# Attention and feed-forward layer on eight cores: one PSUM copy goes to another engine, one wait moves behind the state update

## The chip, the cores and the metric

The kernel runs on all 8 cores of one Trainium2 chip. Each core takes one of the 8 sequences of the batch, with no traffic between cores. The time is the device time of the slowest core, in microseconds; of several runs the median counts.

## The reference

`x` has the shape (8, 8192, 1024). The layer computes, all in float32:

```python
q, k, v = x @ Wq.T, x @ Wk.T, x @ Wv.T          # 8 heads of 128
# causal linear attention without softmax, in chunks:
inter  = q_chunk @ state
scores = (q_chunk @ k_chunk.T) * tril
intra  = scores @ v_chunk
state  = state + k_chunk.T @ v_chunk
o = (inter + intra) / max(|q . cumsum(k)|, 1)
o = rmsnorm(o, norm_w, per head) @ Wo.T
x = layernorm(x + o)
# feed-forward with 8-bit fake-quantised weights and a rank-16 addition
h = gelu(x @ (quant(W_fc) + 2 * B_fc @ A_fc).T + b_fc)
y = h @ (quant(W_proj) + 2 * B_proj @ A_proj).T + b_proj
x = layernorm(x + y)
```

## The kernel before

The program is written for each engine by hand. A small class `Prog` holds one list of instructions per engine and one counting semaphore per engine (`pe`, `ve` for DVE, `ac` for ACT, `gd` and `ld` for the DMAs). `P.wait(engine, token)` puts a wait into that engine's list, `P.op` and `P.close` give the token of an instruction. Every engine works through its list strictly in order, so whatever stands behind a wait waits too. The order of each list is the order in which the Python code emits it.

Pass 1 does the attention. It loops over 16 tiles of 512 rows (`for t in range(NT1)`). Each tile has two phases.

In the first, `qkv_groups` makes 24 groups of eight matmuls (L275 for q and k, L298 for v; 128x512 each) into the three PSUM banks pR0, pR1 and pD, copied out in turns by ACT (L287, L310) and DVE (L284, L307). From the fifth group on, one step of the tail of the tile before is emitted behind each group: `s_sq` (squares on ACT, L322, sums on DVE, L325), `s_dn` (the denominators), then for each of four blocks of 128 rows `s_apply` (L360, DVE scales the block into osq) and `s_wo`. In `s_wo` TensorE transposes the block into pZ (L376) and pSA (L383), two copies bring it to `o2f_sb` (L388 and L391), and TensorE multiplies it by Wo (L401, eight matmuls into pOA and eight into pOB), which waits for both copies. L408 and L412 (DVE) add the input. `s_ssq` (L431, ACT) follows.

In the second phase four chunks of 128 rows pass through the state recurrence. For each chunk TensorE transposes k (L556, into pR0 and pR1) and computes the scores (L565, into pSA and pSB). ACT copies the transposed k to `ktm_sb` (L572, L574). DVE masks the scores (L577, L579) and casts the float32 state to bf16 (L584, token `t_scpy`, `state_f32` to `state_sb`). TensorE then computes the state update from `ktm_sb` and `v_sb` (L595, eight matmuls into pR0 and pR1; L601, the key sums, into pZ), which DVE adds to `state_f32` (L606, L610, L614), and the output of the chunk: q times state (L627, L632), masked scores times v (L641, L647). ACT copies the output (L655, L657, L659). Behind it the late steps of the tile before are emitted: the layer-norm scalars (`s_ln`: DVE L442 to L459, ACT L455) behind chunk 0 and one output each (`s_out`: ACT L469) behind chunks 1, 2 and 3, and one job that finds the maximum of a slice of the feed-forward weights (DMA L247, DVE L249 and L252).

Behind pass 1 the feed-forward weights are quantised while the feed-forward tiles begin (from L763 on), and 32 tiles of 256 rows run through two matmuls (L935, L953). Neither edit touches that part.

Of the kernel before, what the change touches and what calls it, by code (L numbers as in the profile page):

```python
# [77 lines left out]
def later(*toks):  # L78
    out = {}
    for t in toks:  # L80
        if t is None:
            continue
        if isinstance(t, list):
            for tt in t:
                if tt is not None:
                    s, v = tt
                    out[s] = max(out.get(s, -1), v)
            continue
        s, v = t
        out[s] = max(out.get(s, -1), v)  # L90
    return [(s, v) for s, v in out.items()]


def build_program(S=8192, debug=False):
# [32 lines left out]
    P = Prog()  # L127
# [56 lines left out]
    with contextlib.ExitStack() as s1:  # L184
# [27 lines left out]
        pSA, pSB = ps1("pSA"), ps1("pSB")  # L212
# [7 lines left out]
        for Wbuf, Wd in [(WqT, wqT_d), (WkT, wkT_d), (WvT, wvT_d), (WoT, woT_d)]:  # L220
# [10 lines left out]
        fr = {"pR0": None, "pR1": None, "pOA": None, "pOB": None, "pD": None,  # L231
              "pSA": None, "pSB": None, "pZ": None, "ostg": None,
              "o2f": None, "sTm": None,
              "scales": None,
              "ktm": None, "state": None, "osq": [None, None],
              "xtm": [None, None], "r1": [None] * 4, "x1o": [None, None],
              "wst": None, "o1rd": [None, None]}
# [77 lines left out]
        def make_tail(t, xb, oev_toks, dn_toks, msq_gate):  # L315
# [53 lines left out]
            def s_wo(j):  # L369
                def f():  # L370
                    P.wait("tensor", fr["apl", j])
                    P.wait("tensor", fr["o2f"])
                    P.wait("tensor", fr["pZ"])
                    for hh in range(4):
                        P.em("tensor", lambda e, h_=hh, c4=hh:
                             e.matmul(pZ[:, c4 * 128:c4 * 128 + 128],  # L376
                                      osq_sb[j % 2][:, h_ * 128:h_ * 128 + 128],
                                      ident16[:], start=True, stop=True))
                    tk0 = P.close("tensor", "pe")
                    P.wait("tensor", fr["pSA"])  # L380
                    for hh in range(4):
                        P.em("tensor", lambda e, h_=4 + hh, c4=hh:
                             e.matmul(pSA[:, c4 * 128:c4 * 128 + 128],  # L383
                                      osq_sb[j % 2][:, h_ * 128:h_ * 128 + 128],
                                      ident16[:], start=True, stop=True))
                    tk1 = P.close("tensor", "pe")
                    P.wait("scalar", tk0)
                    fr["pZ"] = P.op("scalar", "ac", lambda e: e.copy(  # L388
                        o2f_sb[:, 0:512], pZ[:]))
                    P.wait("scalar", tk1)  # L390
                    fr["pSA"] = P.op("scalar", "ac", lambda e: e.copy(  # L391
                        o2f_sb[:, 512:1024], pSA[:]))
                    fr["o1rd"][j % 2] = ("pe", P.counts["pe"])
                    P.wait("tensor", fr["pZ"])
                    P.wait("tensor", fr["pSA"])
                    P.wait("tensor", fr["pOA"])
                    P.wait("tensor", fr["pOB"])
                    for half, po in [(0, pOA), (1, pOB)]:
                        for h in range(H):
                            P.em("tensor", lambda e, p=po, h_=h, hf=half:  # L400
                                 e.matmul(p[:], o2f_sb[:, h_ * 128:h_ * 128 + 128],  # L401
                                          WoT[:, h_ * D + hf * 512:h_ * D + hf * 512 + 512],
                                          start=(h_ == 0), stop=(h_ == 7)))
                    t_wo = P.close("tensor", "pe")
                    fr["o2f"] = t_wo
                    P.wait("vector", t_wo)
                    P.wait("vector", fr["r1"][j])
                    ra = P.op("vector", "ve", lambda e: e.scalar_tensor_tensor(  # L408
                        r1_sb[j][:, 0:512], pOA[:], 1.0,
                        x_tm[xb][:, j * D:j * D + 512],  # L410
                        OP.mult, OP.add, accum_out=R1(2 * j)[:]))
                    rbt = P.op("vector", "ve", lambda e: e.scalar_tensor_tensor(  # L412
                        r1_sb[j][:, 512:1024], pOB[:], 1.0,
                        x_tm[xb][:, j * D + 512:j * D + 1024],
                        OP.mult, OP.add, accum_out=R1(2 * j + 1)[:]))
                    fr["pOA"] = later(ra)
                    fr["pOB"] = later(rbt)
                    fr["res", j] = later(ra, rbt)
                    if j == CPT - 1:
                        fr["xtm"][xb] = rbt  # L420
                return f
# [95 lines left out]
        for t in range(NT1):  # L517
# [30 lines left out]
            for ic in range(CPT):  # L548
# [33 lines left out]
                if c > 0:  # L582
                    P.wait("vector", fr["state"])
                    t_scpy = P.op("vector", "ve", lambda e: e.tensor_copy(  # L584
                        state_sb[:], state_f32[:]))
                else:
                    t_scpy = later(t_st0, t_stf0)
                P.wait("tensor", ev0)
                P.wait("tensor", ev1)
                P.wait("tensor", fr["pZ"])  # L590
                P.wait("tensor", t_scpy)
                for h in range(H):
                    psb = pR0 if h < 4 else pR1
                    P.em("tensor", lambda e, p=psb, h_=h, i_=ic:
# [23 lines left out]
                fr["pR0"] = t_sadd  # L618
                fr["pR1"] = t_sadd
                fr["pZ"] = t_sadd  # L620
                P.wait("tensor", fr["pOA"])
                P.wait("tensor", fr["pOB"])
                P.wait("tensor", fr["pD"])
# [471 lines left out]
```

How the kernel before makes its waits and increments, by code:

```python
        def f(e, _b=build_fn, _s=sem, _n=n):  # L46
            ins = _b(e)
            ins.then_inc(self.sems[_s], _n)
            return ins
# [22 lines left out]
        def f(e, _s=sem, _v=v):  # L72
            e.wait_ge(self.sems[_s], _v)
```

## Time and profile before

| | us |
|---|---|
| median of 3 runs | 4246.8 |
| fastest of them | 4244.87 |
| the profiled execution | 4246.6 |
| its span, first to last instruction, slowest core | 4245.0 |
| spans of the 8 cores | 4232.5 to 4245.0 |
| TensorE busy | 3357.2 |
| ScalarE (ACT) busy | 1589.2 |
| VectorE (DVE) busy | 1340.4 |

The profile shows the slowest core. PE is TensorE, PEld its weight loads, SP the queue that issues most loads. Busy time is a sum over the whole span. A row of a timeline gives the start, the duration, the engine, the line, the operation with its output and inputs, the number of instructions merged into the row and, in brackets, how long the engine had been idle before it and what ended the wait. The granted clock is a share of 2.4 GHz.

### The profile page before, as it was taken

To read this page: it belongs to the slowest core of one execution; us is meant where nothing else is said; L and a number is where in the kernel's file an instruction comes from. 1 tells how busy PE (TensorE), PEld (TensorE's weight loads), DVE (VectorE), ACT (ScalarE), POOL (GpSimd) and SP (SyncE) were. 2 spreads that over 40 slices of the span, in tenths; PEclk is the share of its full clock that TensorE was granted. 3 is DMA by queue.
4 is the path that set the end of the run, shared out by engine and by line. 5 is a ranking of instruction groups with operands and counts; after the bars stand their busy time and mean duration, and the time that the engine had idled before them with its cause. 6 is when DMAs were issued, how large, how long until landed. Compare 5 with 4: busy or idle time off the path is not lost.

```text
span 4245.0 us, 61567 instructions; the slowest of 8 cores (4232.5 to 4245.0 us)
## 1 busy us (share of the span) xinstructions
PE 3357.2 (79%) x21768; PEld 2021.6 (48%) x21768; DVE 1340.4 (32%) x1970; ACT 1589.2 (37%) x2641; POOL 132.0 (3%) x217
## 2 busy tenths in 40 slices
PE   0877777777777777623469999999999999999997
PEld 0444444444444444301136566566666665665664
DVE  0344444444444444448861111111111111111111
ACT  0233333333333333358863333333333333333332
POOL 0000000000000000000000000000000000000000
PEclk9888888888888888755569999999999999999998
DMA  6222222222222222033420100000001001001000
GB/s 119 50 70 70 70 70 70 70 70 70 70 70 70 70 70 70 35 100 101 105 65 31 41 31 31 36 34 32 31 31 41 31 31 41 31 31 36 34 32 21
DMA packets 77971, 231.30 MB, mean 54 GB/s; under 512 B 7760, under 2 KB 24400, under 8 KB 77664
## 3 DMA queue, kind: packets, MB, share of 16 engines
q1 hardware_dynamic: 36368, 134.80, 10.3%
q0 software_dynamic: 41312, 92.55, 8.2%
q8 instruction: 190, 3.11, 0.3%
q14 instruction: 101, 0.83, 0.1%
HBM read 185.65 MB, written 67.11 MB: 60 GB/s over the span
## 4 chain that ended last, share of the span: by engine, by line
PE 64%; ACT 16%; DVE 10%; issue 5%; DMA 4%; ACTq 0%; DVEq 0%; POOL 0%; SPq 0%; POOLq 0%
PE pH L953 19%; PE pA L935 10%; PE pB L935 10%; PE pR L275 5%; PE pOA L401 4%; PE pOB L401 3%; PE pR L298 3%; PE pD L275 2%; PE pD L298 2%; DVE osq L360 2%; ACT x_fm L917 2%; ACT h L942 2%; DVE rowsA L325 1%; PE pR L595 1%; ACT wstg L798 1%
## 5 line engine op out<-in xcount | busy, mean ns | idle before, releaser
L953 PE MATMUL pH<-WpjT,h 128*128 128x512 bf16 x4096 | 1090.3, 391 | 40.6 <-ACT h L942 40.6
L935 PE MATMUL pA<-x_fm,WfcT 128*128 128x256 bf16 x4096 | 567.8, 285 | 93.9 <-ACT x_fm L917 93.9
L953 PEld LDWEIGHTS pH<-WpjT,h 128*128 128x128 bf16 x4096 | 404.0, 100 | 353.1 <-issue 96.9
L935 PE MATMUL pB<-x_fm,WfcT 128*128 128x256 bf16 x4096 | 566.5, 284 | 0.0
L935 PEld LDWEIGHTS pA<-x_fm,WfcT 128*128 128x128 bf16 x4096 | 414.1, 102 | 275.5 <-issue 122.7
L935 PEld LDWEIGHTS pB<-x_fm,WfcT 128*128 128x128 bf16 x4096 | 416.0, 102 | 170.2 <-issue 7.2
L942 ACT ACTIVATE h<-pA,bfc_sb 128x256 bf16<-128x256 f32 x512 | 242.3, 473 | 644.9 <-PE pA L935 640.9
L942 ACT ACTIVATE h<-pB,bfc_sb 128x256 bf16<-128x256 f32 x512 | 242.3, 473 | 560.9 <-PE pB L935 554.2
L1004 DVE TENSOR_TENSOR r<-pH,x1tm 128x512 f32<-128x512 f32 x128 | 88.6, 692 | 992.6 <-PE pH L993 982.3
L275 PE MATMUL pR<-x_fm,WqT 128*128 128x512 bf16 x768 | 189.4, 403 | 107.2 <-DMA x_fm<-xT 106.9
L595 PE MATMUL pR<-v_sb,ktm_sb 128*128 128x128 bf16 x512 | 61.0, 294 | 225.4 <-DVE state_sb L584 134.8
L401 PE MATMUL pOA<-WoT,o2f_sb 128*128 128x512 bf16 x512 | 176.9, 508 | 75.2 <-ACT o2f_sb L391 75.2
L408 DVE SCALAR_TENSOR_TENSOR r<-pOA,x_tm 128x512 f32<-128x512 f32 x64 | 44.3, 692 | 446.6 <-PE pOB L401 446.6
L275 PEld LDWEIGHTS pR<-x_fm,WqT 128*128 128x128 bf16 x768 | 77.8, 103 | 206.1 <-issue 128.5
L595 PEld LDWEIGHTS pR<-v_sb,ktm_sb 128*128 128x128 bf16 x512 | 46.2, 131 | 235.9 <-issue 235.9
L655 ACT CAST o_stg<-pOA 128x512 bf16<-128x512 f32 x64 | 37.5, 585 | 307.7 <-PE pD L647 307.7
L275 PE MATMUL pR<-x_fm,WkT 128*128 128x512 bf16 x640 | 148.4, 379 | 0.0
L298 PE MATMUL pR<-WvT,x_fm 128*128 128x512 bf16 x640 | 146.0, 379 | 0.0
L401 PEld LDWEIGHTS pOA<-WoT,o2f_sb 128*128 128x128 bf16 x512 | 56.2, 118 | 161.3 <-issue 139.8
L401 PE MATMUL pOB<-WoT,o2f_sb 128*128 128x512 bf16 x512 | 132.1, 404 | 0.0
L310 ACT CAST v_sb<-pR 128x512 bf16<-128x512 f32 x48 | 28.1, 585 | 258.4 <-PE pR L298 258.4
L875 POOL DMA_DIRECT2D y<-out x64 | 42.8, 668 | 2026.9 <-DVE out L870 2019.4
(166 smaller groups left out, 3900.8 us busy)
## 6 DMA issues: line engine op xcount, KB each, us to landing
x_tm<-x SPq DMA_DIRECT2D x16, 2048.0 KB, 9.4
x1s<-x1o POOLq DMA_DIRECT2D x64, 512.0 KB, 3.8
x1tm<-x1s SPq DMA_DIRECT2D x32, 1024.0 KB, 4.8
y<-out POOLq DMA_DIRECT2D x64, 512.0 KB, 3.2
wst_sb<-wfcT SPq DMA_DIRECT2D x32, 512.0 KB, 4.3
x_fm<-xT POOLq DMA_DIRECT2D x16, 1024.0 KB, 10.3
wst_sb<-wprojT SPq DMA_DIRECT2D x32, 512.0 KB, 3.9
wstg<-wfcT SPq DMA_DIRECT2D x32, 512.0 KB, 4.7
```

Source lines behind the costliest of these rows:

```text
L275: e.matmul(pq[:], W[:, d_ * D + h_ * HD:d_ * D + h_ * HD + HD], x_fm[:, d_ * T1:(d_ + 1) * T1], start=(d_ == 0), stop=(d_ == 7)))
L298: e.matmul(pq[:], x_fm[:, d_ * T1 + i_ * 128:d_ * T1 + i_ * 128 + 128], WvT[:, d_ * D + hf * 512:d_ * D + hf * 512 + 512], start=(d_ == 0) ...
L360: ap = P.op("vector", "ve", lambda e: e.tensor_tensor(osq_sb[j % 2][:].rearrange("p (c f) -> p c f", f=128), o_stage[:, j * D:(j + 1) * D] ...
L401: e.matmul(p[:], o2f_sb[:, h_ * 128:h_ * 128 + 128], WoT[:, h_ * D + hf * 512:h_ * D + hf * 512 + 512], start=(h_ == 0), stop=(h_ == 7)))
L408: ra = P.op("vector", "ve", lambda e: e.scalar_tensor_tensor(r1_sb[j][:, 0:512], pOA[:], 1.0, x_tm[xb][:, j * D:j * D + 512], OP.mult, OP. ...
L595: e.matmul(p[:, (h_ % 4) * 128:(h_ % 4) * 128 + 128], ktm_sb[:, h_ * 128:h_ * 128 + 128], v_sb[:, i_ * D + h_ * 128:i_ * D + h_ * 128 + 12 ...
L875: e.dma_start(out=y_d[tt * T2 + ii * 128:tt * T2 + ii * 128 + 128, :], in_=out_sb[ii][:]), 16)
L917: e.copy(x1_fm[:, r_ * 512:r_ * 512 + 512], pq_[:]))
L935: e.matmul(p[:, 0:T2], WfcT[:, d_ * FF + f_ * 128:d_ * FF + f_ * 128 + 128], x1_fm[:, d_ * T2:(d_ + 1) * T2], start=(d_ == 0), stop=(d_ == ...
L942: gel[hb] = P.op("scalar", "ac", lambda e, f_=fc, bb=hb: e.activation(h1_sb[bb][:], (pA if bb == 0 else pB)[:, 0:T2], AF.Gelu, bias=bfc_sb ...
L953: e.matmul(pH[ii * 2 + hf][:], h1_sb[bb][:, ii * 128:ii * 128 + 128], WpjT[:, f_ * D + hf * 512:f_ * D + hf * 512 + 512], start=(f_ == 0), ...
L1004: e.tensor_add(r2_sb[bb][:, ii * D + hf * 512:ii * D + hf * 512 + 512], pH[ii * 2 + hf][:], x1_tm[bb][:, ii * D + hf * 512:ii * D + hf * 5 ...
```

## The change

The first edit moves the copy of pSA in `s_wo` from ACT to DVE. The second takes the wait of TensorE for the bf16 state (`t_scpy`) from the state update, which doesn't read it, and puts it in front of the first matmul that does.

```diff
@@ s_wo @@
                     P.wait("scalar", tk0)
                     fr["pZ"] = P.op("scalar", "ac", lambda e: e.copy(
                         o2f_sb[:, 0:512], pZ[:]))
-                    P.wait("scalar", tk1)
-                    fr["pSA"] = P.op("scalar", "ac", lambda e: e.copy(
+                    P.wait("vector", tk1)
+                    fr["pSA"] = P.op("vector", "ve", lambda e: e.tensor_copy(
                         o2f_sb[:, 512:1024], pSA[:]))
@@ the chunk loop @@
                 P.wait("tensor", ev0)
                 P.wait("tensor", ev1)
                 P.wait("tensor", fr["pZ"])
-                P.wait("tensor", t_scpy)
                 for h in range(H):
...
                 fr["pR0"] = t_sadd
                 fr["pR1"] = t_sadd
                 fr["pZ"] = t_sadd
+                P.wait("tensor", t_scpy)
                 P.wait("tensor", fr["pOA"])
                 P.wait("tensor", fr["pOB"])
                 P.wait("tensor", fr["pD"])
```

By the second edit the lines L595, L601, L606, L610 and L614 become L594, L600, L605, L609 and L613.

DVE's list around the first projection of a tail, before (osq is the scaled block, o2f_sb its transpose, r_0 the residual sum of block 0):

```order
L284 CAST k_sb<-pR 128x512 [waits pe,ve]
L360 TENSOR_TENSOR osq<-o_stg,rowsA 128x1024 [waits ve]
L408 SCALAR_TENSOR_TENSOR r_0,rows<-pOA,x_tm 128x512 [waits pe,ve]
L412 SCALAR_TENSOR_TENSOR r_0,rows<-pOB,x_tm 128x512 [waits ve]
L284 CAST k_sb<-pD 128x512 [waits pe,ve]
```

The same place after the change:

```order
L284 CAST k_sb<-pR 128x512 [waits pe,ve]
L360 TENSOR_TENSOR osq<-o_stg,rowsA 128x1024 [waits ve]
L391 CAST o2f_sb<-pSA 128x512 [waits pe,ve]
L408 SCALAR_TENSOR_TENSOR r_0,rows<-pOA,x_tm 128x512 [waits pe,ve]
L412 SCALAR_TENSOR_TENSOR r_0,rows<-pOB,x_tm 128x512 [waits ve]
L284 CAST k_sb<-pD 128x512 [waits pe,ve]
```

L391 is new in DVE's list, between the scaling of the block and the two additions; it is gone from ACT's, where it stood behind L388.

TensorE's list from the end of one chunk to the output of the next, before:

```order
L565 MATMUL pSA<-q_sb,k_sb 128x128 x4
L565 MATMUL pSB<-q_sb,k_sb 128x128 x3
L565 MATMUL pSB<-q_sb,k_sb 128x128 [waits pe]
L595 MATMUL pR<-v_sb,ktm_sb 128x128 [waits ac,ve]
L595 MATMUL pR<-v_sb,ktm_sb 128x128 x7
L601 MATMUL pZ<-ones_c,ktm_sb 128x1 x7
L601 MATMUL pZ<-ones_c,ktm_sb 128x1 [waits pe]
L627 MATMUL pOA<-state_sb,q_sb 128x128
L632 MATMUL pD<-state_sb,q_sb 128x1
```

The same place after the change:

```order
L565 MATMUL pSA<-q_sb,k_sb 128x128 x4
L565 MATMUL pSB<-q_sb,k_sb 128x128 x3
L565 MATMUL pSB<-q_sb,k_sb 128x128 [waits pe]
L594 MATMUL pR<-v_sb,ktm_sb 128x128 [waits ac]
L594 MATMUL pR<-v_sb,ktm_sb 128x128 x7
L600 MATMUL pZ<-ones_c,ktm_sb 128x1 x7
L600 MATMUL pZ<-ones_c,ktm_sb 128x1 [waits pe]
L627 MATMUL pOA<-state_sb,q_sb 128x128 [waits ve]
L632 MATMUL pD<-state_sb,q_sb 128x1
```

The order of TensorE's instructions is the same; the wait for DVE (`ve`) has moved from the update's first matmul to L627's first, 16 matmuls later.

## Rows read from the trace of the kernel before

**Rows 1.** Busy time by stretch: PE, PEld, DVE, ACT, POOL, clock, DMA share, GB/s

```profile
150.00:1830.00 1680.00, 1280.75 (x8514) 716.17 (x8511) 722.68 (x1241) 570.83 (x930) 49.55 (x76) 0.83 0.24 67
```

**Rows 2.** View of line L595: what ended its engine's idle time, us and times

```profile
  DVE state_sb L584: 134.8, 34
  ACT ktm_sb L574: 90.6, 30
```

**Rows 3.** View by line, whole span, L401: busy us, mean ns, idle before

```profile
L401 PE MATMUL pOA<-WoT,o2f_sb 128*128 128x512 bf16 x512 | 176.9, 508 | 75.2 <-ACT o2f_sb L391 75.2
```

**Rows 4.** Timeline of one tile, chunk 0

```profile
675.57 0.61 PE L556 MATMUL pR<-ident,k_sb 128*128 128x128 bf16 x8
677.00 0.58 ACT L574 CAST ktm_sb<-pR 128x512 bf16<-128x512 f32 x1
678.40 0.70 DVE L584 CAST state_sb<-state_f 128x1032 bf16<-128x1032 f32 x1
679.24 0.79 PE L595 MATMUL pR<-v_sb,ktm_sb 128*128 128x128 bf16 x8 [2.61 <-DVE state_sb L584]
680.09 0.27 PE L627 MATMUL pOA<-state_sb,q_sb 128*128 128x128 bf16 x1
```

**Rows 5.** Timeline of the same tile, chunk 1, and DVE's copy L284 by line

```profile
685.16 0.58 ACT L574 CAST ktm_sb<-pR 128x512 bf16<-128x512 f32 x1
688.31 0.70 DVE L584 CAST state_sb<-state_f 128x1032 bf16<-128x1032 f32 x1
689.15 1.01 PE L595 MATMUL pR<-v_sb,ktm_sb 128*128 128x128 bf16 x8 [5.52 <-DVE state_sb L584]
690.22 0.27 PE L627 MATMUL pOA<-state_sb,q_sb 128*128 128x128 bf16 x1
...
L284 DVE CAST k_sb<-pR 128x512 bf16<-128x512 f32 x48 | 33.2, 692 | 16.4 <-PE pR L275 14.7
```

**Rows 6.** Timeline of the same tile, chunk 2, and the masks of chunk 3

```profile
695.59 0.70 DVE L584 CAST state_sb<-state_f 128x1032 bf16<-128x1032 f32 x1
696.52 0.59 ACT L574 CAST ktm_sb<-pR 128x512 bf16<-128x512 f32 x1
...
701.96 0.63 PE L565 MATMUL pSB<-q_sb,k_sb 128*128 128x128 bf16 x4
702.77 0.69 DVE L577 TENSOR_TENSOR sTm_sb<-pSA,mask_s 128x512 bf16<-128x512 f32 x1 [0.60 <-PE pSB L565]
```

**Rows 7.** Timeline, second projection of the tail in the same tile

```profile
741.66 1.23 DVE L360 TENSOR_TENSOR osq<-o_stg,rowsA 128x1024 bf16<-128x1024 bf16 x1
743.03 0.38 PE L376 MATMUL pZ<-ident,osq 128*128 128x128 bf16 x4 [0.62 <-DVE osq L360]
743.25 0.53 PE L383 MATMUL pSA<-ident,osq 128*128 128x128 bf16 x4
743.56 0.58 ACT L388 CAST o2f_sb<-pZ 128x512 bf16<-128x512 f32 x1 [0.41 <-PE pZ L376]
744.23 0.58 ACT L391 CAST o2f_sb<-pSA 128x512 bf16<-128x512 f32 x1
744.96 1.89 PE L401 MATMUL pOA<-WoT,o2f_sb 128*128 128x512 bf16 x8 [1.18 <-ACT o2f_sb L391]
```

**Rows 8.** Timeline of TensorE, the same tile: groups of L275 and L401, next tile's start

```profile
708.65 4.38 PE L275 MATMUL pR<-x_fm,WqT 128*128 128x512 bf16 x16
714.59 3.62 PE L275 MATMUL pR<-x_fm,WqT 128*128 128x512 bf16 x16
733.24 3.57 PE L401 MATMUL pOA<-WoT,o2f_sb 128*128 128x512 bf16 x8 [1.12 <-ACT o2f_sb L391]
754.58 3.57 PE L401 MATMUL pOA<-WoT,o2f_sb 128*128 128x512 bf16 x8 [1.18 <-ACT o2f_sb L391]
781.41 0.61 PE L556 MATMUL pR<-ident,k_sb 128*128 128x128 bf16 x8
```

**Rows 9.** Busy time by stretch, same tile, columns as in rows 1

```profile
730.70:737.50 6.80, 5.28 (x19) 2.27 (x20) 0.26 (x1) 1.17 (x2) 0.00 (x0) 0.50 0.01 2
```

## The prediction

> **What bounds the kernel now.** I read the stretches by time first. Pass 1 (attention) lasts from 105 to about 1830 us, and from 150 on TensorE is busy for 1281 of 1680 us at a mean granted clock of 0.83 [rows 1]. Behind it lie the quantisation of the weights and the feed-forward pass. Only pass 1 holds the two edits. Its 16 tiles follow one another every 105.8 us: L556 of chunk 0 starts at 675.57 and that of the next tile at 781.41 [rows 4, 8]. TensorE is the engine whose idle time counts there. The views by line say what it waits for: before the state update L595 it is idle 134.8 us until the DVE cast of the state (L584, 34 times) and 90.6 us until the ACT copy L574 (30 times) [rows 2]; before the output projection L401 it is idle 75.2 us, all 64 times until the second ACT copy L391 [rows 3]. The timelines of one tile then show what each wait is made of.
>
> **Part one: the copy of pSA goes from ACT to DVE.** It removes 64 ACT copies of 0.58 us and adds 64 DVE copies. The same operation on the same shape, L284 (f32 PSUM to bf16 SBUF, 128x512), takes 0.69 us on DVE (mean 692 ns) against 0.58 us for L391 on ACT [rows 5, 7]. So the copy is longer by 0.11 us, but it no longer queues behind L388. In the second projection of the tile at 675 the transposes into pSA end at 743.25 + 0.53 = 743.78, L388 begins at 743.56, L391 at 744.23, and L401 at 744.96, which is 1.18 us after the transposes [rows 7]. From the end of a TensorE group to the DVE row that waits for it there are 0.18 us (L565 ends at 702.59, L577 starts at 702.77), and from a DVE end to TensorE 0.14 us (L360 ends at 742.89, L376 starts at 743.03) [rows 6, 7]. The new gap is 0.18 + 0.69 + 0.14 = 1.01 us. L388 ends at 744.14 and is no longer late. Over the 64 gaps: 75.2/64 = 1.175, less 1.01 = 0.165, times 64 = 10.6 us. The new copy stands right behind L360 in DVE's order. L360 ends at 742.89, before the transposes start, and L408, next in line, waits for the projection anyway, so nothing is held up on DVE. Its price is bounded by 0.58 and by 1.2 us (a DVE row of 1024 elements, L360); I take 0.69 from the row of the same shape. The other ends would make the term 17 us or minus 22 us.
>
> A rule speaks against this edit. The Trainium skill ("VectorE: DVE Perf Modes", Specifications) puts ScalarE closer to PSUM and VectorE closer to SBUF, and its errata section prices a PSUM-to-SBUF operation of 512 elements at (120 + 512)/0.96 = 658 ns on VectorE and (172 + 512)/1.2 = 570 ns on ScalarE. By the page the new gap would be 0.98 us and the term 12.5 us. The order of the two agrees with the rows (0.69 and 0.58), the sizes are a little low.
>
> **Part two: the wait for the state cast moves behind the update.** L595 and L601 (the update, now L594 and L600) read only ktm_sb and v_sb. They can start when ACT has made ktm_sb; the state cast is needed at L627. No instruction is added; one wait moves by 16 matmuls. Per chunk, what can be won is the smaller of two spans: how much later L584 ends than L574, and how long L595 and L601 run before L627.
> Chunk 0 of the tile at 675: L574 ends at 677.58, L584 at 679.10 (1.52 later), L595 starts at 679.24 and L627 at 680.09 [rows 4]. The update moves into the idle 1.5 us, L627 comes at 679.24, and 0.85 us are won. Chunk 1: L574 ends at 685.74, L584 at 689.01 (3.27 later; DVE has the layer-norm scalars, the 1.22 us maximum and the masks in front), L595 starts at 689.15, L627 at 690.22: 1.07 us are won [rows 5]. Chunks 2 and 3: L584 ends before L574 (696.29 against 697.11), since ACT writes x1 (L469) before it copies, so nothing is won [rows 6]. This pattern repeats in every tile. Summed chunk by chunk: 15 chunks 0 give 12.9 us, 16 chunks 1 give 17.1, three chunks of the first tile and the last 2.1, together 34 chunks (the 34 waits of rows 2) and 32.1 us. Of 134.8 us of idle time only a quarter goes, because the state cast stays late and L627 now waits for it.
> What is queued behind the moved wait: L627 to L647, and then ACT's copies of the output, which start the next chunk. They waited for the same cast before, so none gets later. DVE's L606 gets earlier, since the update is done when the cast ends. The bounds of this part are 0 (should the weight loads in front of L627 be dear once they wait) and 35 us; I take 32.1. If chunks come sooner, DVE's weight maximum (L249) may come to wait for its slice, but the cast that it would delay has the update, up to 1.07 us, as cover [rows 5].
>
> **The clock.** TensorE runs at 1.2 or 2.4 GHz, and the rows of the same eight matmuls show both: L401 into pOA takes 1.89 us at 744.96 and 3.57 us at 733.24 and 754.58; the first 16 of L275 take 4.38 us against 3.62 us later [rows 7, 8]. The stretch 730.7 to 737.5 has a granted clock of 0.50 [rows 9]. In each case TensorE had idled: 2.5 us before L376 at 731.1; 0.61 and 1.18 us around the transposes before 754.58. In 14 of the 16 tiles the third projection's group takes 3.23 to 3.57 us, as the one at 754.58 does, which costs 14 x 1.65 = 23 us. The first L275 pair (16 matmuls) takes about 4.5 us in 14 tiles, which costs 14 x 0.87 = 12 us. The first projection's group is slow in all tiles and will stay so, as the 2.5 us in front of it stay. The third is a near thing, since the second and fourth have the same two gaps and run at 2.4 GHz. With the gap 0.17 us shorter and the tile's start about 2 us earlier I expect half of those 23 us back: 12 us. The bounds are +35 (both kinds gone) and -35: all of L275's first 16 matmuls at 1.2 GHz in every tile, which costs 16 x 0.21 - 0.87 = 2.5 us, 14 times.
>
> **Sum.** 10.6 + 32.1 + 12 = 54.7 us. The profiled execution took 4246.6 us (span 4245.0), the median is 4246.8, so nothing is to be shifted: 4192 us.
>
> **The rivals.**
> The clock gives it back (0.20). The tile period is the same to some tenths of a microsecond in all 16 tiles, though chunks arrive with scatter. Work that comes earlier may only stand longer at 1.2 GHz before the clock rises: in the tile at 675 it rises at about 710, TensorE having been busy without a gap since L595 at 705.4; L275, started 1.9 us earlier, could then run 3.3 us at half clock in place of 1.35, which gives back 1.0 us per tile, and the projections another 0.7. Then 42.7 - 16 x 1.7 = 15 us remain: 4231 us. The Trainium skill ("TensorE: Matmul & The Clock Gate", Part 1) says that the clock is halved by default and that sustained activity releases it; by that rule removed idle time and moved work change the clock too, in a direction that the rule alone does not give.
> The waits only shift (part of my forecast's range): 42.7 us and no clock effect, 4204 us.
> More than forecast (0.08): both slow groups run at 2.4 GHz in most tiles. 42.7 + 35 = 78: 4169 us or less.
> Slower (0.04): the update now runs alone, with idle time in front of it and behind it, and TensorE has no unbroken stretch before L275. If the clock then stays at 1.2 GHz through the first 16 matmuls of L275 (+2.5 us per tile), and the first projection's pOB too (8 x 0.21 = 1.7 us less the 0.5 it pays already, +1.2), that is 3.7 x 16 = 59 us against 42.7: 4263 us. It decides from 2.7 us per tile on. For it speaks that pass 1 as a whole has a clock of only 0.83 [rows 1]; against it, that L594 to L647 of chunk 3 stay unbroken, as no cast is late there.
> The change doesn't do what it says: L594 still waits for DVE, or the DVE copy stands behind a late row. The order of instructions excludes the first, and rows 7 the second.
>
> **How the numbers follow.** Forecast with the plain shift 0.68, clock gives back 0.20, more 0.08, slower 0.04. The range that holds 8 in 10 goes from 4168 to 4226: below it most of the "more" case, above it the harder half of the give-back and the slower case. A measurement of this kernel tells about 2% from no change, 85 us: faster than 4162 needs more than all slow groups gone, 0.04; slower than 4332 has no mechanism with a price near it, 0.01; within, 0.95.
>
> **What would show it.** L391 as a DVE row of 0.69 us that starts 0.18 us after L383 ends, and L401 1.0 us behind it: idle before L401 near 65 us. L594's idle time named after ACT in chunks 0 and 1, and new idle time before L627 named after L584, about 0.45 us in chunk 0 and 2.2 us in chunk 1. Tile period 102 to 103.5 us in place of 105.8. Feed-forward stretch as long as before. Wrong would be: a period of 105 us or more with the waits gone (then the clock), L401 more than 1.1 us behind the transposes, or L627 later than L584's end by over 0.3 us.

## The result and the profile after

The changed kernel takes 4162.5 us (median of 8 runs, 4151.7 to 4178.0) against 4247.1 us before: the ratio is 0.980, with a 95% interval of 0.9781 to 0.9819. That is 85 us less, where 55 were forecast, and 5.5 us under the lower end of the range. The profiled execution took 4165.6 us with a span of 4164.0. Some executions run with one die at a lower granted clock and take some per cent longer; the ratios leave these out, and for the experiments the ratio and the time of the profiled execution are given in place of a median.

First the stretch table of the changed kernel, in the columns of [rows 1], to be read against that row.

```profile
150.00:1750.00 1600.00, 1240.92 (x8529) 689.14 (x8527) 767.16 (x1302) 532.20 (x866) 49.46 (x75) 0.87 0.26 71
```

Pass 1 is 80 us shorter (it ended at about 1830 us and ends at about 1750). TensorE executes the same number of matmuls in it, but is busy for 40 us less, and the mean granted clock has gone from 0.83 to 0.87. So about half of the gain is waiting that went away (399 us idle before, 359 after); the other half is the same matmuls run faster. The busy time of the feed-forward lines is unchanged, L953 at 1090 us for example.

Next, what TensorE waited for in pass 1 (total us, number of times, longest), after:

```profile
PE pR L594 <- ACT ktm_sb L574: 134.4, 64, 3.5
PE pZ L376 <- DVE osq L360: 91.3, 64, 14.1
PE pOA L401 <- DVE o2f_sb L391: 65.2, 64, 1.4
PE pOA L627 <- DVE state_sb L584: 55.6, 35, 4.3
PE pR L556 <- DVE state_f L613: 6.0, 15, 0.8
```

The same view of the kernel before, so that the sums can be compared:

```profile
PE pR L595 <- DVE state_sb L584: 134.8, 34, 5.8
PE pR L595 <- ACT ktm_sb L574: 90.6, 30, 3.6
PE pZ L376 <- DVE osq L360: 90.3, 64, 14.1
PE pOA L401 <- ACT o2f_sb L391: 75.2, 64, 1.5
PE pR L556 <- DVE state_f L614: 1.1, 2, 0.8
```

The five rows of each add up to 352.5 and 392.0 us: 39.5 us less waiting. L401 lost 10.0 us of it, as forecast (10.6). The update lost 91.0 us, of which 55.6 came back in front of L627, and L556 waits 4.9 us more for the additions into `state_f32`: 30.5 us net, where 32.1 were forecast. Both waits came close to what the prediction said.

The first two chunks of the tile that starts at 654 us show the mechanism against [rows 4] and [rows 5]:

```profile
655.76 0.59 ACT L574 CAST ktm_sb<-pR 128x512 bf16<-128x512 f32 x1
656.49 0.61 PE L594 MATMUL pR<-v_sb,ktm_sb 128*128 128x128 bf16 x8 [1.10 <-ACT ktm_sb L574]
657.16 0.70 DVE L584 CAST state_sb<-state_f 128x1032 bf16<-128x1032 f32 x1
658.00 0.22 PE L627 MATMUL pOA<-state_sb,q_sb 128*128 128x128 bf16 x1 [0.72 <-DVE state_sb L584]
659.86 0.61 PE L556 MATMUL pR<-ident,k_sb 128*128 128x128 bf16 x8 [0.40 <-DVE state_f L613]
...
662.26 0.59 ACT L574 CAST ktm_sb<-pR 128x512 bf16<-128x512 f32 x1
663.00 0.61 PE L594 MATMUL pR<-v_sb,ktm_sb 128*128 128x128 bf16 x8 [2.08 <-ACT ktm_sb L574]
665.41 0.70 DVE L584 CAST state_sb<-state_f 128x1032 bf16<-128x1032 f32 x1
666.25 0.27 PE L627 MATMUL pOA<-state_sb,q_sb 128*128 128x128 bf16 x1 [2.47 <-DVE state_sb L584]
```

The update starts 0.14 us after ACT's copy and L627 0.14 us after the cast. What the prediction left out is the duration: L594 now takes 0.61 us where L595 took 0.79 and 1.01. In chunk 0 L627 starts at 658.00 and the next chunk's L556 could start at 659.46, had it not waited 0.40 us for DVE. In the kernel before, L627 to L556 took 2.21 us in that place (680.09 to 682.30). The granted clock of chunk 0 is 1.00 in this tile (654.34 to 659.86), and was 0.79 in the tile of [rows 4] (675.57 to 682.30). One tile does not say which of the two edits did that; e1, e2 and e9 below do.

The projection, to be read against [rows 7] (first five rows) and [rows 8] (the last two, a first projection and a third one, which took 3.57 us each before):

```profile
714.99 0.53 PE L383 MATMUL pSA<-ident,osq 128*128 128x128 bf16 x4
715.30 0.59 ACT L388 CAST o2f_sb<-pZ 128x512 bf16<-128x512 f32 x1 [0.41 <-PE pZ L376]
715.69 0.69 DVE L391 CAST o2f_sb<-pSA 128x512 bf16<-128x512 f32 x1 [1.07 <-PE pSA L383]
716.53 1.89 PE L401 MATMUL pOA<-WoT,o2f_sb 128*128 128x512 bf16 x8 [1.01 <-DVE o2f_sb L391]
...
L401 PE MATMUL pOA<-WoT,o2f_sb 128*128 128x512 bf16 x512 | 155.6, 458 | 65.2 <-DVE o2f_sb L391 65.2
...
707.09 1.89 PE L401 MATMUL pOA<-WoT,o2f_sb 128*128 128x512 bf16 x8 [1.01 <-DVE o2f_sb L391]
725.98 1.89 PE L401 MATMUL pOA<-WoT,o2f_sb 128*128 128x512 bf16 x8 [1.01 <-DVE o2f_sb L391]
```

The gap is 1.01 us to the hundredth, and the DVE copy runs beside the end of the ACT copy. L401 into pOA is busy 155.6 us against 176.9 in [rows 3], 21 us less. All four projections of this tile run at 2.4 GHz, even the first behind its idle 2.5 us; the forecast said that the first would stay slow everywhere. This tile is a rare one, though. A pOA group takes 1.89 us at 2.4 GHz. The first projections do so in 2 of the 16 tiles (in none before) and take 3.03 to 3.57 us in the other 14. The third projections are slow in 4 of the 16 tiles, and were so in 15.

Per tile, from the first L556 to the next tile's (14 tiles each, without the first and last): before 105.9 us, in a band of 105.7 to 106.2; after 100.8 us, in a band of 96.6 to 103.9. Cut at the first L275, the chunk phase went from 32.8 to 29.8 us and the projection phase from 73.1 to 71.0 us.

### The profile page after: what moved, and what is told of

Same layout as the page of the kernel before. It is cut to its first block, busy times and chain, and to the rows that moved or that the text cites. A ratio compares the mean times of both kernels' runs of the same rounds, so it can differ in the third digit from the quotient of the medians.

```text
span 4164.0 us, 61567 instructions; the slowest of 8 cores (4137.9 to 4164.0 us)
## 1 busy us (share of the span) xinstructions
PE 3316.6 (80%) x21768; PEld 1992.8 (48%) x21768; DVE 1385.0 (33%) x2034; ACT 1553.6 (37%) x2577; POOL 132.7 (3%) x217
## 4 chain that ended last, share of the span: by engine, by line
PE 64%; ACT 14%; DVE 12%; issue 5%; DMA 5%; ACTq 0%; DVEq 0%; SPq 0%; POOL 0%; POOLq 0%
PE pH L953 19%; PE pA L935 10%; PE pB L935 10%; PE pR L275 5%; PE pOA L401 4%; PE pOB L401 3%; PE pR L298 3%; PE pD L275 2%; PE pD L298 2%; DVE osq L360 2%; ACT x_fm L917 2%; ACT h L942 2%; DVE rowsA L325 1%; DVE o2f_sb L391 1%; ACT out L837 1%
## 5 line engine op out<-in xcount | busy, mean ns | idle before, releaser
L953 PE MATMUL pH<-WpjT,h 128*128 128x512 bf16 x4096 | 1090.4, 391 | 39.2 <-ACT h L942 39.2
L953 PEld LDWEIGHTS pH<-WpjT,h 128*128 128x128 bf16 x4096 | 403.6, 100 | 351.5 <-issue 94.9
L275 PE MATMUL pR<-x_fm,WqT 128*128 128x512 bf16 x768 | 187.9, 401 | 109.8 <-DMA x_fm<-xT 108.9
L401 PE MATMUL pOA<-WoT,o2f_sb 128*128 128x512 bf16 x512 | 155.6, 458 | 65.2 <-DVE o2f_sb L391 65.2
L275 PEld LDWEIGHTS pR<-x_fm,WqT 128*128 128x128 bf16 x768 | 77.4, 102 | 208.1 <-issue 129.7
L594 PE MATMUL pR<-v_sb,ktm_sb 128*128 128x128 bf16 x512 | 46.3, 243 | 134.4 <-ACT ktm_sb L574 134.4
L275 PE MATMUL pR<-x_fm,WkT 128*128 128x512 bf16 x640 | 148.4, 379 | 0.0
L401 PE MATMUL pOB<-WoT,o2f_sb 128*128 128x512 bf16 x512 | 131.5, 403 | 0.0
L401 PEld LDWEIGHTS pOA<-WoT,o2f_sb 128*128 128x128 bf16 x512 | 52.1, 110 | 138.2 <-issue 107.3
```

What stands on the lines that cost most here:

```text
L275: e.matmul(pq[:], W[:, d_ * D + h_ * HD:d_ * D + h_ * HD + HD], x_fm[:, d_ * T1:(d_ + 1) * T1], start=(d_ == 0), stop=(d_ == 7)))
L401: e.matmul(p[:], o2f_sb[:, h_ * 128:h_ * 128 + 128], WoT[:, h_ * D + hf * 512:h_ * D + hf * 512 + 512], start=(h_ == 0), stop=(h_ == 7)))
L594: e.matmul(p[:, (h_ % 4) * 128:(h_ % 4) * 128 + 128], ktm_sb[:, h_ * 128:h_ * 128 + 128], v_sb[:, i_ * D + h_ * 128:i_ * D + h_ * 128 + 12 ...
L953: e.matmul(pH[ii * 2 + hf][:], h1_sb[bb][:, ii * 128:ii * 128 + 128], WpjT[:, f_ * D + hf * 512:f_ * D + hf * 512 + 512], start=(f_ == 0), ...
```

## The experiments

Three theories stood at first, and further rivals are named in the expectations. Theory A: the waits are one term and the clock another, which answers to small amounts of idle time. Rival B: the whole clock gain hangs on the state update's edit. Theory C (also called rival C): the clock holds the tile period fixed.

**e1: the first edit alone.**

```diff
-                    P.wait("scalar", tk1)
-                    fr["pSA"] = P.op("scalar", "ac", lambda e: e.copy(
+                    P.wait("vector", tk1)
+                    fr["pSA"] = P.op("vector", "ve", lambda e: e.tensor_copy(
```

> The kernel before with the first edit alone (the pSA copy on DVE). Theory A (the waits are one thing, TensorE's clock another that the shorter idle gap can switch): idle before L401 falls from 75.2 to about 65 us, and the third projection's pOA groups, 3.5 us in 14 tiles before, mostly run in 1.89 us; 10.6 + up to 23 us, so 4215 to 4230 us. Rival B (only the waits shorten, the clock change of the whole comes with the state update's edit): 4236 us, third projections as slow as before. Rival C (the tile period is held by the clock): within 3 us of before.

Measured: ratio to before 0.988 (0.9807 to 0.9956), 4209 us profiled. View by line:

```profile
L401 PE MATMUL pOA<-WoT,o2f_sb 128*128 128x512 bf16 x512 | 151.2, 449 | 65.1 <-DVE o2f_sb L391 65.1
```

The time is below the 4215 to 4230 us that theory A gave. The waits in front of L401 shrink by 10 us as computed; the span shrinks by 37 (4245.0 to 4207.6), while L401's own time falls by 26 us. The span understates the gain, because the first L556 of this core comes only at 161.2 us, against 149.6 before: cores 4 to 7 of the same profile take 4180.3 to 4192.6 us, and took 4232.5 to 4245.0. The third projections are slow in 3 of 16 tiles, in place of 15, and the tile period falls from 105.9 to 102.3 us: rivals B and C fall.

**e2: the second edit alone.**

```diff
                 P.wait("tensor", fr["pZ"])
-                P.wait("tensor", t_scpy)
                 for h in range(H):
...
                 fr["pZ"] = t_sadd
+                P.wait("tensor", t_scpy)
                 P.wait("tensor", fr["pOA"])
```

> The kernel before with the second edit alone (the wait for the state cast behind the update). Theory A: TensorE's idle time in front of the update and of L627 falls by about 32 us against 225 us in all, tile periods spread, time 4195 to 4215 us, and L401 keeps its gap of 1.18 us with third projections slow in at least half of the tiles. Rival B (the clock gain of about 41 us belongs to this edit): 4170 to 4180 us. Rival C (the clock holds the period at 105.8 us): over 4235 us.

Measured: ratio 0.986 (0.9822 to 0.9899), 4196 us profiled.

Two rows by line and, below the dots, one of TensorE's waits:

```profile
L401 PE MATMUL pOA<-WoT,o2f_sb 128*128 128x512 bf16 x512 | 165.3, 481 | 75.8 <-ACT o2f_sb L391 75.8
L594 PE MATMUL pR<-v_sb,ktm_sb 128*128 128x128 bf16 x512 | 46.4, 243 | 132.6 <-ACT ktm_sb L574 132.6
...
PE pOA L627 <- DVE state_sb L584: 52.1, 33, 3.3
```

Some 50 us are gained, 41 of them waits in front of the update and of L627 (225.4 us before, 132.6 + 52.1 now). The gap of L401 is untouched (75.8), yet its busy time falls by 12 us, as more of the groups fall on high clock. The chunk phase falls from 32.8 to 30.1 us, but by idle time alone. The update's matmuls take 243 ns in place of 294, yet the scores (L565 into pSA) take 285 in place of 245 and the transposes of k (L556) 283 in place of 269: TensorE is busy for 18.34 us of a chunk phase, against 18.45 before.

The two edits do not simply add up. The tile period falls by 3.5 us with the first alone, by 3.7 with the second alone, and by 5.1 with both. The waits nearly add (TensorE's idle time per tile falls by 0.5 and 2.5 us alone, 2.6 together); the time that it is busy does not (3.1 and 1.1 us alone, 2.5 together).

**e9: one idle gap filled, no wait removed.** This is the decisive run, since it has neither of the change's two edits. It puts one matmul whose result is overwritten into each gap between the transposes and L401. That matmul writes pOA, so a wait for pOA's last reader is added in front of the transposes; the idle time there stays at 90.3 us.

```diff
+        def warm(n):
+            for _ in range(n):
+                P.em("tensor", lambda e: e.matmul(
+                    pOA[:], ident16[:], WoT[:, 0:512], start=True, stop=True))
...
+                    P.wait("tensor", fr["pOA"])
...
                     tk1 = P.close("tensor", "pe")
+                    warm(1)
```

> The kernel before with one thrown-away matmul (128x512) in each gap between the transposes and L401, and nothing else. It takes no wait away and makes the idle part of the gap 0.22 us shorter, about as much as the moved copy does (0.17 us). Theory A (a slightly smaller idle share keeps the clock up): third projections mostly at 1.89 us, L401 into pOA 150 to 160 us busy, time 4205 to 4225 us. Rival F (only a shift of the tile's start does it): L401 stays at 177 us and the time at 4247 us.

Measured: ratio 0.988 (0.9855 to 0.9899), 4199 us profiled. L401 stands on line 409 here:

```profile
L409 PE MATMUL pOA<-WoT,o2f_sb 128*128 128x512 bf16 x512 | 146.5, 437 | 59.3 <-ACT o2f_sb L399 59.3
```

The kernel before does 64 extra matmuls and is nearly 50 us faster, more than theory A's 4205 to 4225 us. L401 still waits for both copies on ACT and starts no earlier behind the transposes (1.18 us on average in both kernels); only its idle time is 16 us less, by the extra matmuls' own time. Its pOA groups are 30 us shorter, and the third projection is slow in one tile of 16. The chunk phase, in which nothing was changed, has TensorE busy for 17.38 us in place of 18.45. This shows theory A without any of the change's savings in it: the clock term alone, from one small gap, is as large as the waits that the change removes. The tile periods spread here too (100.3 to 104.4 us after the first).

**e6: the gap made long again.** To the changed kernel a DVE memset of 128x4 is added (into a new buffer), for which L401 waits.

```diff
+                    fr["pSA"] = P.op("vector", "ve", lambda e: e.memset(
+                        wtmp2[:, 0:4], 0.0))
```

> The changed kernel with a small DVE memset (128x4) behind the pSA copy for which L401 waits: the gap before L401 becomes about 1.28 us in place of 1.01. Waits alone: 64 x 0.27 = 17 us, so 4180 us. Theory A (the shorter gap is what keeps the third projection at 2.4 GHz): its pOA groups are slow again in most tiles, L401 into pOA rises from 155.6 to about 175 us busy, time 4195 to 4210 us. Rival F (the tile's start relative to the clock decides, not the gap): L401 stays near 156 us and the time near 4180 us.

Measured: ratio 0.988 (0.9857 to 0.9892), 4194 us profiled. L401 is line 404:

```profile
L404 PE MATMUL pOA<-WoT,o2f_sb 128*128 128x512 bf16 x512 | 168.1, 488 | 77.7 <-DVE wtmp L394 77.7
```

The gap grew by 0.20 us, which is 12.5 us of waiting, and the span grew by 28 (4164.0 to 4192.0). The third projections are slow again in 13 of 16 tiles, as theory A expected and rival F did not. L401's pOA busy time rose by 12.5 us only, between the two (175 and 156), because the first projections now take 2.75 to 2.97 us in nine tiles. The chunk phase has TensorE busy for 18.20 us again. So the gap decides most of it; why the first projections moved was not traced.

TensorE by tile, mean of the 14 inner tiles of the slowest core in us; a projection counts as slow when its pOA group takes more than 2.5 us:

| kernel | chunk phase | TensorE busy in it | rest of the tile | TensorE busy in it | first projections slow | third slow |
|---|---|---|---|---|---|---|
| before | 32.8 | 18.45 | 73.1 | 63.94 | 16 of 16 | 15 of 16 |
| e1, copy alone | 31.9 | 17.49 | 70.4 | 61.85 | 14 | 3 |
| e2, wait alone | 30.1 | 18.34 | 72.1 | 62.92 | 15 | 12 |
| e9, gap filled | 32.0 | 17.38 | 70.7 | 62.50 (with the four extra matmuls) | 12 | 1 |
| after | 29.8 | 17.45 | 71.0 | 62.44 | 14 | 4 |
| e6, gap long again | 30.0 | 18.20 | 72.5 | 63.12 | 16 | 13 |
| e3, before with gaps filled (below) | 32.2 | 18.10 | 68.8 | 66.52 (with the extra matmuls) | 1 | 1 |

The busy time of the chunk phase holds on every core: 18.38 to 18.45 us before, 18.32 to 18.44 in e2, 17.23 to 17.92 in e1, 17.38 to 17.66 in e9 and 17.10 to 17.50 after. So the faster matmuls of the chunk phase do not come with the moved wait: e2 has it and lacks them, e1 and e9 have them without it, with nothing changed but the gap in the other phase of the tile. A smaller idle time there is not enough by itself either, since e3 and e7 (below) lack most or all of them. What decides is not shown; the rows show the granted clock of chunk 0, 0.79 on average before and 0.93 to 0.96 in e1, e9 and after.

**e5: a delay added to the kernel before** (the state cast issued twice).

```diff
                     t_scpy = P.op("vector", "ve", lambda e: e.tensor_copy(
                         state_sb[:], state_f32[:]))
+                    t_scpy = P.op("vector", "ve", lambda e: e.tensor_copy(
+                        state_sb[:], state_f32[:]))
```

> The kernel before with the state cast L584 issued twice, so that it ends 0.8 us later in every chunk. Its casts come last in chunks 0 and 1 and nearly last in 2 and 3 (0.55 and 0.06 us before ACT), so the waits alone give 0.8 + 0.8 + 0.25 + 0.74 = 2.6 us per tile. Theory C (the clock holds the period of the kernel before at 105.8 us, by giving time back or taking it): tile periods stay within 0.5 us of 105.8, time under 4260 us. Rival D (waits add up plainly): 4288 us, all periods about 108.4 us. Rival E (more idle time also costs clock): over 4300 us.

Measured: ratio 1.012 (1.0098 to 1.0134), 4298 us profiled.

```profile
L597 PE MATMUL pR<-v_sb,ktm_sb 128*128 128x128 bf16 x512 | 64.4, 305 | 265.2 <-DVE state_sb L586 264.1 <-ACT ktm_sb L574 1.1
```

The idle time in front of the update rose by 39.8 us, against 41.6 by the expectation's 2.6 us for 16 tiles, and the span by 51 (4245.0 to 4296.2). So theory C falls in the form that the time is held: waits come through in full, with about 11 us of slower matmuls on top (TensorE is busy for 3369.3 us, against 3357.2). The periods are as even as before, though (109.1 to 109.6 us in 14 of the 15), 3.4 us above those of before for 2.6 us of added wait.

**e3 and e4: the idle gaps of the projections filled,** before and after the change: `warm(4)` in the gap, `warm(10 if j == 0 else 2)` in front of L376.

> The kernel before with matmuls whose result is thrown away (identity times Wo into pOA, before pOA is written anew): four in each gap between the transposes and L401, two in front of L376 (ten at the first projection of a tile). No wait is removed. Theory A (idle gaps switch the clock): all L401 groups take 1.89 us; 23 us from the third and about 34 us from the first projections come back, so 4185 to 4200 us. Rival B (the clock follows something else than these gaps): L401 as before and the time the same or up to 20 us longer.

> The changed kernel with the same filling matmuls. Theory A: L401 into pOA falls from 155.6 us busy to about 121 us and the time to 4125 to 4140 us. Rival B: same as the changed kernel or slower. If it is above 4162 us while L401 is at 1.89 us, the clock loss has moved to another stage, above all to L275's first groups.

Measured: e3 has the ratio 0.981 (0.9774 to 0.9841), 4174 us profiled; e4 0.970 (0.9646 to 0.9755), 4120 us profiled. L401 in e3, then in e4:

```profile
L409 PE MATMUL pOA<-WoT,o2f_sb 128*128 128x512 bf16 x512 | 124.0, 386 | 20.1 <-ACT o2f_sb L399 20.1
```

```profile
L409 PE MATMUL pOA<-WoT,o2f_sb 128*128 128x512 bf16 x512 | 124.6, 387 | 9.0 <-DVE o2f_sb L399 2.4
```

Both profiled times are below what theory A expected, so it was too careful. L401 into pOA needs 124 us when it is nearly always at 2.4 GHz, so the half clock cost 53 us in the kernel before (176.9) and 32 us in the changed one (155.6), the pOB half (132.1 to 120.9) another 11. The matmuls in front of the first projection cover its idle 2.5 us too.

**e7: the projection in two parts.** Heads 0 to 3 need only the copy of pZ.

```diff
-                    P.wait("tensor", fr["pSA"])
...
-                    for half, po in [(0, pOA), (1, pOB)]:
-                        for h in range(H):
+                    for part, half, po in [(0, 0, pOA), (0, 1, pOB),
+                                           (1, 0, pOA), (1, 1, pOB)]:
+                        if part == 1:
+                            P.wait("tensor", fr["pSA"])
+                        for h in range(4 * part, 4 * part + 4):
```

> The changed kernel with the projection in two parts: heads 0 to 3 into pOA and pOB wait only for the copy of pZ, heads 4 to 7 for that of pSA. The gap before L401 falls from 1.01 to about 0.5 us. Waits alone: 64 x 0.5 = 32 us, 4130 us. Theory A adds clock: 4115 to 4130 us, with L401 busy in all below 270 us. Rival: the waits are given back by the clock, over 4145 us.

Measured: ratio to before 0.976 (0.9733 to 0.9789), the two fastest of the three runs compared 4135 us, the third 4165. The row is of core 4, whose span is 4122.0 us:

```profile
PE pOA L403 <- ACT o2f_sb L388: 32.4, 64, 0.8
```

The waiting in front of the projection halves, from 65.2 to 32.4 us, as computed. The time is at the figure of the waits alone (4130) or a little above; the extra clock that theory A expected did not come. L403 is busy for 265.7 us in all on this core, under the 270 of theory A, but the trace lacks 32 of its 1024 matmuls, so that says little; the first projection is slow in 15 of 16 tiles, and the chunk phase has TensorE busy for 18.55 us.

**e12: split and fill together,** with two filling matmuls in the gap in place of four.

> The changed kernel with the split projection and the filling matmuls alone. e4 (fill alone) ran in about 4122 us and e7 (split alone) in about 4135 us. Added up from 4162: 4095 us. Rival: both remove the same idle time of the same gap, so that it stays at 4110 to 4120 us.

Measured: ratio 0.962 (0.9595 to 0.9639), 4089 us profiled, span 4087.0: better than both kernels and the best of this study, 158 us below the kernel before and 74 below the changed one.

```profile
PE pR L604 <- ACT ktm_sb L584: 134.1, 64, 3.0
PE pOA L637 <- DVE state_sb L594: 51.1, 33, 2.8
PE pZ L383 <- DVE osq L365: 29.1, 64, 8.5
```

L411 (the projection) no longer appears among the long waits (6.3 us in front of pOA); what is left lies in the chunk phase, in front of the update (L604, 134.1 us) and of the first output matmul (L637, which is L627 before; 51.1 us). The rival that both remove the same idle time (4110 to 4120 us) falls.

**e8, e10, e11: three attempts at the late cast, all misses.** e8 put the cast behind the end of the chunk before and the weight maximum behind the masks; e10 moved the maximum jobs into the projection phase; e11 joined e10, the early cast, the split and the fill. The lines below are the added ones; the old cast and the old place of the jobs are taken out.

```diff
# e8 and e11: behind fr["state"] = t_omm
+                P.wait("vector", t_omm)
+                t_scpy_next = P.op("vector", "ve", lambda e: e.tensor_copy(
+                    state_sb[:], state_f32[:]))
# e8: the job behind the masks, in front of L606
+                jj = 4 * t + ic
+                if jj < len(wmax_jobs):
+                    emit_wmax_job(wmax_jobs[jj])
# e10 and e11: the jobs behind projection groups
+                if gi in (16, 18, 20, 22):
+                    emit_wmax_job(wmax_jobs[4 * t + (gi - 16) // 2])
```

> The changed kernel with the state cast right behind the end of the chunk before (it waits for that chunk's last matmul), and the weight maximum behind the masks. Idle time before L627 (55.6 us) goes nearly to zero. Waits alone: about 50 us less, 4112 us. Theory A: the chunks' matmuls run at 2.4 GHz more often, 4095 to 4112 us. Rival: the masks L577 and L579 become the late ones at L641 and take half of it, 4130 to 4145 us.

> The changed kernel with the weight-maximum jobs (L249, L252) taken out of the chunk loop and put behind projection groups 16, 18, 20 and 22 of the tile, where DVE idles. The cast in chunk 1 then comes 1.4 us earlier and less stands in front of it elsewhere. Idle time before L627 falls from 55.6 to about 30 us; waits alone 4135 us; with the clock 4110 to 4150 us.

> The changed kernel with the maximum jobs moved as above, the state cast directly behind the end of the chunk before, the projection split in two parts and filling matmuls (two in the gap, ten or two in front of L376). If the parts add up: 4162 less 25 (jobs), 25 (rest of the cast's lateness), 30 (split) and 35 (fill): about 4045 us. If the clock and ACT's copies take half of it: 4090 us.

Measured: e8 0.991 (0.9896 to 0.9925), 4207 us profiled, slower than the changed kernel and than even the rival of its expectation. The waits of TensorE tell why:

```profile
PE pR L556 <- DVE state_f L614: 116.8, 48, 5.6
PE pR L595 <- ACT ktm_sb L574: 89.0, 64, 2.6
```

The idle time in front of L627 is gone, but the maximum (1.22 us) now stands in DVE's list in front of the additions L606 to L614, and L556 of the next chunk waits for them. In 16 of the 64 chunks the maximum in turn waits for its slice of weights (50.8 us in all, up to 4.5), and these chunks carry the longest waits of L556. The late cast was traded for late additions; the masks, which the rival named, are not what waits. e10: 1.014 (1.011 to 1.0165), slower than the kernel before. DVE's waits:

```profile
DVE wtmp L249 <- DMA wst_sb<-wfcT: 112.9, 22, 10.5
DVE wtmp L249 <- DMA wst_sb<-wprojT: 100.5, 24, 9.5
```

The job has one staging buffer, so each load starts only after the maximum before it. In the chunk loop, 8 us lie between jobs and the load is hidden (a single wait of 1.8 us before). With two groups between jobs DVE waits 213 us, and the copies out of PSUM stand behind it. e11 carries the same fault and came to 0.988 (0.9849 to 0.9919), 4198 and 4207 us, where 4045 or 4090 were expected. What the early cast is worth without that fault was not measured.

## Why the prediction was wrong

Both waits were forecast well. "Part one": 10.6 us forecast, 10.0 us measured; the 0.69 us copy, the times on either side (0.17 and 0.15 us, forecast 0.18 and 0.14) and the gap of 1.01 us came as computed, and the wait for the scaled block in front of L376 grew by 1.0 us only. "Part two": 32.1 us forecast, 30.5 us measured; the idle time did reappear in front of L627, in 35 chunks. There it was 0.72 us in chunk 0 and 2.47 us in chunk 1 of one tile, against 0.45 and 2.2 forecast, because the update itself ran shorter than it had. The maximum L249 did come to wait for its slice, as the prediction thought possible: 24 us in 15 waits, against a single one of 1.8 us before.

The step that failed is the term called "The clock": 12 us forecast, some 41 us measured (81.0 us of span less 39.5 us of waits; TensorE's busy time, 3357.2 us before and 3316.6 after, says the same). Three things were wrong in it.

The third projections: "I expect half of those 23 us back". They were slow in 15 tiles and not in 14, and took 24.3 us more than at 2.4 GHz; after the change they take 5.4 us more. So 18.9 us came back where 12 were forecast. e9 shows that 0.2 us of idle time less in that gap is enough by itself, without either edit.

The first projections: "will stay so, as the 2.5 us in front of it stay". The 2.5 us did stay (in the tile shown, L376 waits 2.53 us), and the first projections mostly stayed slow: 2 of the 16 now take 1.89 us and two more a little less than before, which is 4.2 us in all. That they vary at all goes with the spread of the periods (96.6 to 103.9 us); whether it comes from when the tile arrives there is not shown. e3 shows the full price of half clock in L401: 53 us into pOA, not the 23 us counted; the other 30 us, which the forecast gave up as not to be had, are mostly those of the first projections (26.9 us), and filling matmuls did get them back.

The chunk phase: the term contained nothing for it. Its matmuls were counted at their old durations. Per tile the chunk phase fell by 3.0 us, of which 2.0 are idle time and 1.0 is TensorE's busy time (18.45 to 17.45 us), some 15 us in all. The update's matmuls show it most (294 to 243 ns, 61.0 to 46.3 us busy), but they mislead about its source: they fell to 243 ns in e2 too, where the whole phase gained nearly nothing, and e1 and e9 have the whole 1.0 us without the second edit. What decides whether the phase gains stays open, as e3 and e7 show. With L401's 21 us this makes 36 of the 41 us.

The other group that the term counted hardly moved. The first 16 matmuls of L275 take 68.8 us in 15 tiles before and 66.0 after: 2.8 us of the 12 that the bound held for them, where the forecast itself counted none.

The rival "the clock gives it back" was given 0.20 for an argument from the even periods. The result is against it, since more time went than the waits, and e5 answers the argument: the periods are even under a delay too, but the time is not held. Why some kernels of this study have even periods (before, e5) and others uneven ones (after, e1, e9) stays open, and so does why e5's 2.6 us of wait became 3.4 us of period.

The rival "more than forecast" (0.08, 4169 us or less) has the right number, and that is luck: it took L275's first groups to rise to 2.4 GHz, which they did not, and had nothing for the chunk phase.

The bounds held the truth badly for a reason that can be named: +35 us was called the bound of the clock term, from two groups of rows that were slow, while pass 1's granted clock of 0.83 already said that more than these two groups ran at half clock. With the two levels 0.5 and 1.0, a mean of 0.83 is about a third of the 1680 us at the lower one, some 570 us (an estimate from [rows 1]); the two kinds of groups last some 110 us together (14 times 3.5 and 4.5 us).

## What to carry to other kernels

Where TensorE idles in short gaps between groups, price the granted clock of the whole stretch (here 0.83 over 1680 us), not only the wait: a gap changed by 0.2 us was worth 10 to 16 us of idle time and 15 to 50 us of clock (e6, e1, e9). The price can fall in another phase than the one that was edited: compare busy time by phase before giving it to an edit, and not one line's mean, which in e2 fell while its neighbours rose. Before any reordering, try a matmul that is thrown away in the gap; e9 costs a few lines and gives nearly 50 us, and e12 (fill and split on top of the change) is 158 us faster than the kernel before. And when a wait is moved behind work that doesn't need it, count the idle time that comes back. Of the 134.8 us until the cast, 43.8 came back in the same place as waiting for ACT (90.6 to 134.4 us) and 55.6 in front of L627.

## What was not expected of the hardware

That 64 extra matmuls of 128x512, of 0.38 to 0.63 us each, make the kernel nearly 50 us faster (4199 against 4247 us), and that 1.07 us per tile of what they save lies in the chunk phase, where none of them stands. That a 128x512 matmul of L401 takes 379 to 387 ns on average when nearly all run at 2.4 GHz (e3, e4), where the mean into pOA was 508 ns before. And that the spread between runs rises with the change: 4244.9 to 4247.8 us for the kernel before in the first comparison, 4151.7 to 4178.0 us for the changed kernel, whose cores spread from 4137.9 to 4164.0 us in the profiled execution (before: 4232.5 to 4245.0), all with the same instructions.
